# A decoder layer on one core: another order for TensorE's small operations in causal attention

## The reference, cut to what matters

```python
def attn(x, Wq, Wk, Wv, Wo):          # x: 4 batches, T = 512 tokens, D = 512, 16 heads of 32
    q, k, v = ((x @ W).reshape(B, T, 16, 32) for W in (Wq, Wk, Wv))
    scores = einsum('bthd,bshd->bhts', q, k) * tril(ones(T, T))   # masked entries are 0, not -inf
    attn = softmax(scores / T ** 0.5)
    return einsum('bhts,bshd->bthd', attn, v).reshape(B, T, D) @ Wo
x = x + attn(layernorm(x), Wq, Wk, Wv, Wo)
x = x + xattn(layernorm(x), ctx, ...)    # a second attention over a context
x = x + ffn(layernorm(x), ...)           # gate, up and down weights of 4 bits, unpacked with scales
```

## Time and profile before

| | us |
|---|---|
| median of 3 runs | 1482.5 (1481.33 to 1483.2) |
| the profiled execution, its own time | 1482.48 |
| its span in the profile | 1480.8 |
| TensorE busy | 1426.6 (96%) |
| attention steps of the first batch, from the scores of unit 1 to the next norm's transposes | 70.26 to 128.06 |
| the same of the second, third and fourth batch begin at | 202.19, 334.33, 470.88 |

### The profile page before, as it was taken

One profiled execution on the slowest core, in us unless ns is written; L12 is line 12 of the kernel. 1 busy time (PEld: TensorE's weight loads), 2 busy tenths in 40 slices (PEclk: granted clock), 3 DMA queues, 4 the chain that ended last, 5 costly groups with the idle time before them and its releaser, 6 DMA issues.

```text
span 1480.8 us, 26838 instructions
## 1 busy us (share of the span) xinstructions
PE 1426.6 (96%) x8896; PEld 720.5 (49%) x8896; DVE 990.7 (67%) x2125; ACT 716.4 (48%) x1660; POOL 380.2 (26%) x691
## 2 busy tenths in 40 slices
PE   6989998998998899999999999999999999999999
PEld 4465456556644654344444444444444444444444
DVE  7786688678668767887566666655765765665533
ACT  5795279239615945254353353353343442533432
POOL 0053225304363436512211112112112212212100
PEclk9999999999999999999999999999999999999999
DMA  7554522352454521000000001001001001000011
GB/s 249 136 166 125 155 86 81 111 163 66 147 154 137 195 81 45 17 16 33 22 13 32 17 17 33 17 17 35 17 17 32 17 16 33 17 17 1 0 58 57
DMA packets 76877, 98.01 MB, mean 66 GB/s; under 512 B 8000, under 2 KB 60736, under 8 KB 76224
## 3 DMA queue, kind: packets, MB, share of 16 engines
q1 hardware_dynamic: 76736, 96.23, 21.2%
HBM read 68.94 MB, written 27.26 MB: 65 GB/s over the span
## 4 chain that ended last, share of the span: by engine, by line
PE 83%; DVE 5%; issue 5%; ACT 4%; POOL 1%; DMA 1%; ACTq 0%; POOLq 0%; SPq 0%; DVEq 0%
PE bank L876 24%; PE bank L877 24%; PE bank L878 24%; PE bank L940 2%; ACT prob L1257 2%; PE bank L961 2%; PE bank L1016 1%; PE bank L929 1%; PE bank L889 1%; PE bank L970 1%; PE bank L1011 1%; PE bank L1001 1%; DVE xt L1585 1%; DMA pk_in<-L_ffn_down_W_packed_dram 1%; ACT prob_t L1273 1%
## 5 line engine op out<-in xcount | busy, mean ns | idle before, releaser
L876 PE MATMUL bank<-xs,G 128*128 128x512 f16 x896 | 339.8, 379 | 2.0 <-DVE c L1730 0.9
L878 PE MATMUL bank<-xs,G 128*128 128x512 f16 x896 | 339.6, 379 | 0.0
L877 PE MATMUL bank<-xs,G 128*128 128x512 f16 x896 | 339.6, 379 | 0.0
L1345 ACT COPY c<-bank 128x512 f32<-128x512 f32 x192 | 111.2, 579 | 220.0 <-PE bank L878 215.2
L1730 DVE TENSOR_TENSOR c<-bank,c 128x512 f32<-128x512 f32 x128 | 88.1, 689 | 193.0 <-PE bank L878 193.0
L876 PE MATMUL bank<-Wd,hid 128*128 128x512 f16 x512 | 194.1, 379 | 2.8 <-DVE X L1784 2.8
L878 PE MATMUL bank<-Wd,hid 128*128 128x512 f16 x512 | 194.0, 379 | 0.0
L877 PE MATMUL bank<-Wd,hid 128*128 128x512 f16 x512 | 194.0, 379 | 0.0
L748 POOL TENSOR_TENSOR c<-c,m 128x512 f32<-128x512 f32 x64 | 82.4, 1287 | 388.5 <-ACT c L1345 388.5
L1784 DVE SCALAR_TENSOR_TENSOR X<-bank,col,X 128x512 f32<-128x512 f32 x128 | 95.4, 750 | 101.5 <-PE bank L878 101.4
L1600 DVE CUSTOM_DVE_ANT_0 bank<-bank,mask,col 128x128 f32<-128x128 f32 (+3 forms) x256 | 139.1, 548 | 23.0 <-issue 17.8
(11 more groups left out here) (192 smaller groups left out, 2409.1 us busy)
## 6 DMA issues: line engine op xcount, KB each, us to landing
stack<-qk_dram SPq DMA_DIRECT2D x128, 128.0 KB, 3.3
sc_in<-scale_t SPq DMA_DIRECT2D x30, 384.0 KB
qk_dram<-qk SPq DMA_DIRECT2D x32, 256.0 KB, 2.9
packed_t<-pk_t SPq DMA_DIRECT2D x32, 192.0 KB, 1.9
pk_in<-packed_t SPq DMA_DIRECT2D x30, 192.0 KB
X<-in_x_dram SPq DMA_DIRECT2D x4, 1024.0 KB, 5.7
pk_in<-L_ffn_gate_W_packed_dram SPq DMA_DIRECT2D x16, 256.0 KB, 2.7
pk_in<-n_L_ffn_up_W_packed_dram SPq DMA_DIRECT2D x16, 256.0 KB, 3.0
```

What stands on the lines that cost most here:

```text
L876: pe.matmul(o, lhs(0), rhs(0), start=first, stop=False, skip_group_check=onto)
L877: pe.matmul(o, lhs(0), rhs(1), start=False, stop=False, skip_group_check=onto)
L878: return pe.matmul(o, lhs(1), rhs(0), start=False, stop=stop, skip_group_check=onto)
L1345: nc.scalar.copy(dst[:], bank[BANK_Y if which == M5 else x][:]).then_inc(c_copied, 1)
```

## The change

On PE, `recips` of the unit before moves from behind the fourth head of a step to behind the second, and `values` of the unit before, which stood behind the fourth head in one piece, is cut in two: one half behind the third head and one behind the fourth (for step 15 both stay behind the second head, undivided). The two halves of `repack` stood in one row behind the second head of steps 4, 8 and 12. Now the first half stands behind the first head of that step, the second half behind the first head of the step after it. The slot numbers follow. ACT takes `recip_out` two heads earlier, and DVE copies the second packed half one unit later.

```diff
         def turn_slot(h):
-            return h + 2 * (max(0, h - 2) // 16) + max(0, h // 4 - 1)
+            recips_past = max(0, h - 2) // 4
+            packs_past = sum(h > 16 * (r + 1) + 4 * half for r in range(HG - 1) for half in range(2))
+            return h + recips_past + packs_past
...
-        AT_RECIP, AT_DIVIDE = 9, 12
+        AT_RECIP, AT_DIVIDE = 7, 12
...
-            def values(n, u):
+            def values(n, u, parts=(0, 1)):
 
                 hg, i = u // TT, u % TT
+                total = wide[i] // P + (i < TT - 1)
+                ks = range(0 if 0 in parts else total // 2, total if 1 in parts else total // 2)
...
-                for k in range(blocks + (i < TT - 1)):
+                for k in ks:
...
-            def repack(n, r):
+            def repack(n, r, half):
...
+                        if j == 1 and u > 0:
+                            recips(n, u - 1)
                         if j == 1 and u == UNITS - 1:
                             values(n, u - 1)
-                        if j == 3 and u > 0:
-                            recips(n, u - 1)
-                            if u < UNITS - 1:
-                                values(n, u - 1)
-                        if j == 1 and u % TT == 0 and u > 0:
-                            repack(n, u // TT - 1)
-                repack(n, HG - 1)
+                        if j > 1 and 0 < u < UNITS - 1:
+                            values(n, u - 1, (j - 2,))
+                        if j == 0 and u % TT < 2 and u >= TT:
+                            repack(n, u // TT - 1, u % TT)
+                repack(n, HG - 1, 0)
+                repack(n, HG - 1, 1)
...
-                        if j == 0 and u % TT == 1 and u > TT:
+                        if j == 1 and u % TT == 2 and u > TT:
                             repacked(n, u // TT - 1)
```

More of the change, by code:

```diff
@@ L296, in pack_slot @@
         def pack_slot(r, half):
-            return (turn_slot(16 * r + 17) + 1 if r < HG - 1 else recip_slot(UNITS - 2) + 1) + half
+            return turn_slot(16 * (r + 1) + 4 * half) + 1 if r < HG - 1 else turn_slot(ROWS - 1) + 1 + half
         def recip_slot(u):
-            return turn_slot(4 * u + 7) + 1 if u < UNITS - 1 else pack_slot(HG - 1, 1) + 1
+            return turn_slot(4 * u + 5) + 1 if u < UNITS - 1 else pack_slot(HG - 1, 1) + 1
         def turn_bank(slot):
@@ L953, in values @@
                 at = P * (u % 2)
-                if i < TT - 1:
+                if i < TT - 1 and 1 in parts:
                     pe.wait_ge(v_zero_done, beyond_units(n, u))
-                for k in range(blocks + (i < TT - 1)):
+                for k in ks:
                     for j in range(4):
@@ L961, in values @@
                         mm = pe.matmul(bank[6][32 * j:32 * j + 32, at:at + P], lhs, rhs, start=(k == 0), stop=(k == blocks - (i == TT - 1)))
-                mm.then_inc(av_done, 1)
+                if 1 in parts:
+                    mm.then_inc(av_done, 1)
             def recips(n, u):
@@ L1023, in context_out @@
                     mm.then_inc(att_full, 1)
-            def repack(n, r):
+            def repack(n, r, half):
                 nb = n * (NB // B) + r
                 pe.wait_ge(pk_conv, 6 * nb + 6)
[L1028 to L1037, removed]
+                pe.wait_ge(*turn_read(n, pack_slot(r, half) - 3))
+                bk = turn_bank(pack_slot(r, half))[:].bitcast(F16)
+                tiles = [[(0, 0), (1, 0)], [(0, 1), (1, 1)], [(2, 0), (3, 0)]] if half == 0 else \
+                        [[(2, 1), (3, 1)], [(4, 0), (4, 1)], [(5, 0), (5, 1)]]
+                for q in range(3):
+                    for e, (a, w) in enumerate(tiles[q]):
+                        mm = pe.transpose(bk[:, 256 * q + P * e:256 * q + P * e + P], pk_16[:, a, P * w:P * w + P], ident16[:])
+                mm.then_inc(pk_full, 1)
             def product(m, x, which, pair, slot, nb):
```

## The result

The changed kernel takes **1490.45 us** (median of 5 runs, 1489.14 to 1490.93), the kernel before 1482.5 (1481.33 to 1483.2). The ratio is 1.005, with a 95% interval of 1.0039 to 1.0061: slower by 8 us, where 6 were forecast. The profiled execution has a span of 1488.7 us, 7.9 above that of before.

A forecast was written before the change was run, and what follows sets the result against it. No engine was taken as full in the attention, all near. A period of four units was to grow from 15.12 to 15.69 us; three batches gave +4.9, batch 4 about +1.2, together +6.1: 1488.5 us, range 1478.5 to 1495.

The forecast's parts named there:

- the last link: From the copy of turn 11.1 to scores 13.0: a shorter block stands behind the waiting turn; 2.08 to 1.87 us, -0.21.
- The price of a visit: PE's passage into the 128x32 tiles (0.09 us) and out (0.11): 0.20 per visit, three visits a step instead of one.
- the first link: From scores 9.0 (unit 9, head 0) to scores 10.0: turn 8.2 waits for ACT's packed copy; 3.61 to 3.76 us, +0.15.
- the third link: From exp 11.0 to the copy of turn 11.1: four maxima and exponentials of 512, unchanged at 3.77 us.
- The hidden 0.15: Between scores 10.0 and exp 11.0: ACT had been busy until 107.95, which hid 0.15 us of the maximum's 0.78 lateness.
- the second link: From scores 10.0 to exp 11.0: DVE's late packed copy delays turn 9.2 and the maximum of 10.3; 5.66 to 6.29, +0.63.
- A batch: First group -0.3, two whole periods +1.14, last group +0.15 and +0.63: sum +1.62 us, for three batches +4.9.
- (1): Rival: changing tiles costs nothing when weights are loaded ahead; 14.89 us per period, about 1479.6 in all; chance 0.13.
- (2): Rival: the copy of the second packed half is not late; a period gains 0.06, about 1481.5 us; chance 0.13.
- rival 3: Free tile changes and a copy not late together: 0.65 us gained in each of eleven periods, 1474.5; chance 0.07.
- (4): Rival: PE becomes the bound, each visit to the tiles costing 0.4 us; 0.8 more per period, 1497; chance 0.07.
- the signs: Trace marks of the forecast, among them periods of 15.6 to 15.8 us and `out_tail` 0.6 later behind scores 10.0 than 4.17.

The follow-up runs named there:

- packed halves alone: The kernel before with only the two packed halves moved as in the change, reciprocals as before and values whole: 1488.48 us, 15.57 per period.
- the repeated waits: The kernel before with only the packed halves moved, plus three already met waits written again in the middle of each whole values: 1484.89 us.
- halves alone: The kernel before with only the values cut in two, behind third and fourth head; reciprocals and packed halves as before: 1475.59 us.
- `out_tail` first: The kernel before with only the values cut in two, and POOL's `out_tail` ahead of the convert in step 10: 1473.65 us.
- both mends: The changed kernel with DVE's copy of the second packed half one maximum earlier and POOL's `out_tail` ahead of the convert: 1481.31 us.
- packed halves put back: The changed kernel with both packed halves and DVE's copy back in their old places, reciprocals and halved values as changed: 1480.88 us.
- the copy one maximum earlier: The changed kernel with DVE's copy of the second packed half one maximum earlier, PE's order untouched: 1485.51 us.

## Why the prediction was right, point by point

- **What can move.** Right: the two passages of 74.12 us and the feed-forward part are as before. That the loss reaches the end whole was wrong by 2.5 us: 1.67 by the clock of the two profiled executions, and 0.80 by PE's stop in the feed-forward part, which no kernel with as many instructions as the change shows.
- **The waits.** Right, each: turn 8.2 behind ACT's copy, turn 9.2 behind DVE's 2.57 after scores 10.0 (forecast 2.58), the maximum of 10.3 at 3.79 (3.73). Making turn 9.2 0.6 earlier gave 0.41 per period back. What ACT was to gain in the last link came (1.90, forecast 1.87), but a new wait of 0.34 stands in the second.
- **The price of a visit.** Too small, a term of the sum. Turn to values is 0.34 us (105.96 to 106.30), of which two turns are 0.22: 0.12 in. Values to scores is 0.36 (106.30 to 106.66), of which four products are 0.22: 0.14 out. Together 0.26, not 0.20; the two visits of the first link took 0.25 and 0.23. The old rows had `recips` and the values side by side; a block by itself costs more. By the Trainium skill (TensorEngine Tiling, Key Properties) a change of the tiling mode drains the engine. The trace agrees that it costs time, 0.23 to 0.26 us for the two ways. Over the three visits of the first two links that is 0.14 more; from the maximum to the exponential came another 0.07 (2.63 against 2.56), and 0.11 in the third link, where exp 11.1 starts 1.22 behind exp 11.0 and not 1.11. With 0.03 in the last link these are, within 0.01, the 0.36 by which a period is longer than forecast.
- **The hidden 0.15.** A second term of the sum, and also too small. The forecast took 0.15 off the second link, since ACT had been busy until exp 11.0, and left the third, counted from exp 11.0, at its old 3.77. But exp 11.1 hangs on the division. In the kernel before:

```profile
109.06 0.72 ACT L1257 ACTIVATE prob<-bank,nmx 128x512 f32<-128x512 f32 x1
```

That is 1.35 behind the division at 107.71, and in the changed kernel it is 1.35 again (109.68 to 111.03). Exp 11.0 stood 0.24 behind the division before and stands 0.13 behind it now. So what was gained up to exp 11.0 is lost again up to exp 11.1: this is the 0.11.
- **A batch.** Forecast +1.62, measured +2.91 in the first. The first group gave 0.16 and not 0.3, two periods lost 1.86 and not 1.14, and from scores 13.0 on 1.21 were lost and not 0.78. That last is the surplus of the first two links (0.24 + 0.76), and 0.2 behind them, which I had put at nothing; 0.19 of it lies between exp 15.0 and exp 15.1, which start 1.22 apart and not 1.03 as before.
- **Batch 4.** Forecast +1.2, measured +1.47. As foreseen its first period hid its loss behind POOL's old wait: up to scores 9.0 the batch gained 0.28, forecast 0.2. The second period lost 0.93 and not 0.57, the rest 0.82 (0.78).
- **The rivals.** Changing tiles was not free (1). The second packed copy was late (2), so 3 is out as well. PE is 0.79 us busier per period, some 0.10 for each of the eight visits more, but a visit costs 0.26 and not 0.4, and kernels with eight visits per period lie between 14.57 and 15.82 us, those with twelve between 15.20 and 16.05: PE isn't the bound (4). The 1474.5 of rival 3 doesn't follow from its own terms: eleven times 0.65 from 1482.5 gives about 1475.4.
- **The number.** 1490.45 against 1488.5. The terms came to 6.1 us and the attention lost 10.3, so the sum was nearer than its terms, by the 2.5 us that came back outside the attention. That nearness was luck. Two of the signs were missed in size: a period is 16.05 and not 15.6 to 15.8, and `out_tail` starts 5.04 behind scores 10.0, 0.87 later and not 0.6 (the forecast's own maximum would have made it 0.78).

Still open: how the reciprocals' 0.25 per period divides between the longer waits and the new visits, and why the packed halves alone cost 0.45.

## What to carry to other kernels

Where buffers are given out in turn, moving one small operation moves the waits of all that stand behind it: write down, for each taker, which copy it waits for and when that copy is made, before and after. A wait is cheap behind the last issue of a step and dear ahead of it. And take a change in parts, by a stretch of the trace and not by the time alone: here the parts give -3.7, +1.7 and +4.4 us of attention by themselves and +10.3 together, and a stop hundreds of us later moved a time by 3.6 us.

## What the hardware showed that I had not expected

- **A stop of PE that moves with the number of instructions**: 0.8 to 2.9 us in the feed-forward part, whose code no edit touches, gone when waits that cost nothing were added in the attention, more than 400 us earlier. In packed halves alone the clock behind it was 0.50 (1.2 GHz) in one stretch of 2 us and 0.69 in the next; the whole end was 4.3 us longer than with the repeated waits.
- **The clock.** After the same 2.7 us of waiting PE was granted half its clock in one profile and the whole in another. The passage between batches 3 and 4 took 77.05 to 77.09 us in four profiles (the change, halves alone, `out_tail` first, both mends) and 78.72 to 78.80 in the ten others, and nothing in between. By the Trainium skill (TensorE: Matmul & The Clock Gate, Part 1) the monitor that sets the clock doesn't start with the kernel, so that one kernel can differ at its start from one execution to the next. Here executions of one kernel differ as well: with the packed halves put back, four at a mean clock of 1.000 took 1479.35 to 1480.47 us, four at 0.998 took 1482.13 to 1482.79 (the other two, at 0.999 and 0.997, 1480.11 and 1481.29). The order may bear on how often it happens: the mean clock was 0.999 or more in all five executions of the changed kernel, and in 34 of the 83 of the kernel before that were timed beside the experiments. No run settles that. At the same mean clock, 0.999, the changed kernel takes 1490.46 on average (four executions) and the kernel before 1482.01 (ten, beside the run with the copy one maximum earlier): 8.5 us.
- **Tiles.** A passage from the whole array to 128x32 tiles and back costs 0.20 us where the small operations lie in a row (104.26 to 105.05 in the earlier trace rows), and 0.23 to 0.26 where one stands alone (101.69 to 103.39 and 105.96 to 106.66 in the changed kernel).
